# Attention logits of a graph network: four groups' head sums in four quarters of the partitions, and the edges' product filled up with zero rows

## What is computed

```python
x_l = (x @ W_l).reshape(n, H, C)          # H = 8 heads, C = 16
x_r = (x @ W_r).reshape(n, H, C)
e = (ea @ W_e).reshape(-1, H, C)          # ea: 32 features of each edge
m = leaky_relu(x_l[src] + x_r[dst] + e, 0.2)
alpha = einsum('ehc,hc->eh', m, att)      # 8 logits of each edge
amax = segment_max(alpha, dst)
expa = exp(alpha - amax[dst])
out = segment_sum(x_l[src] * a[:, :, None], dst)   # a = expa / sum of expa
```

## Time and profile before

| | |
|---|---|
| time, median of 3 runs | 2102.23 us (2099.22 to 2106.14) |
| the profiled execution: time | 2107.33 us |
| its span, first to last instruction | 2105.5 us |
| mean granted TensorE clock | 0.884 |
| PE busy | 1848.9 us (88%) |
| VectorE busy | 1373.9 us (65%) |
| ScalarE busy | 1035.5 us (49%) |
| GpSimd busy | 844.7 us (40%) |

### The profile page before, as it was taken

How to read it: one execution, slowest core, us unless ns; L and a number is a source line. 1 busy time by engine, 2 the same in 40 slices (tenths; PEclk the granted TensorE clock), 3 DMA queues, 4 the chain that set the end, 5 groups by cost and what they waited for, 6 DMA issues and landing times. The chain is left out here.

```text
span 2105.5 us, 35427 instructions
## 1 busy us (share of the span) xinstructions
PE 1848.9 (88%) x10749; PEld 1210.7 (58%) x10749; DVE 1373.9 (65%) x3215; ACT 1035.5 (49%) x2285; POOL 844.7 (40%) x884
## 2 busy tenths in 40 slices
PE   5677789997999997789999999999999999998856
PEld 2567765556888775335555555555555555555545
DVE  6999967775533335686666666666666666567775
ACT  0588877754642344124545454444545454543325
POOL 2000000001000000577777777777777777775200
PEclk9655569998999999779999999999999999998877
DMA  3100000001520001333333333333333333333111
GB/s 97 43 2 2 2 9 0 1 20 38 148 85 1 6 1 35 92 89 88 97 96 95 94 95 94 94 93 95 94 92 91 93 92 92 96 87 81 34 36 31
DMA packets 132536, 133.24 MB, mean 63 GB/s; under 512 B 29098, under 2 KB 102403, under 8 KB 132355
## 3 DMA queue, kind: packets, MB, share of 16 engines
q1 hardware_dynamic: 104578, 73.76, 12.1%
q0 software_dynamic: 27776, 57.20, 11.1%
HBM read 126.05 MB, written 4.82 MB: 62 GB/s over the span
## 5 line engine op out<-in xcount | busy, mean ns | idle before, releaser
L2203 POOL DMA_INDIRECT rows<-x_l,src x856 | 821.4, 960 | 309.5 <-issue 250.9
L2330 ACT ACTIVATE bent<-psum 128x512 f32<-128x512 f32 x214 | 126.8, 593 | 379.9 <-PE psum L2230 372.8
L2291 PEld LDWEIGHTS psum<-both,node_hot 128*128 128x128 f32 x1712 | 247.0, 209 | 83.2 <-issue 72.6
L2291 PE MATMUL psum<-both,node_hot 128*128 128x144 f32 x1712 | 293.1, 321 | 0.0
L2388 DVE TENSOR_TENSOR bent<-psum,bent 128x512 f32<-128x512 f32 x214 | 147.6, 690 | 195.0 <-ACT bent L2330 194.5
L2345 ACT ACTIVATE apart<-iota,rel 128x128 bf16<-128x128 f32 x796 | 252.9, 388 | 9.2 <-PE psum L2291 7.6
L2221 PEld LDWEIGHTS psum<-hot,x_r_parts 128*128 x1284 | 115.2, 100 | 235.5 <-issue 219.7
L2224 PE MATMUL psum<-edges,w_e 32*128 32x512 f32 x428 | 247.2, 658 | 0.1
L2241 PE MATMUL psum<-bent,att_heads 128*64 128x512 f32 (+2 forms) x428 | 243.8, 665 | 0.0
L2221 PE MATMUL psum<-hot,x_r_parts 128*128 128x256 bf16 x1284 | 187.4, 282 | 50.0 <-DVE hot L2384 49.1
L2481 DVE TENSOR_TENSOR acc<-acc,psum 128x144 f32 x428 | 128.8, 301 | 134.1 <-PE psum L2291 95.9
(11 more groups left out here) (343 smaller groups left out, 2396.7 us busy)
## 6 DMA issues: line engine op xcount, KB each, us to landing
rel_row<-e_rel_rows SPq DMA_DIRECT2D x107, 256.0 KB
edges<-edge_t SPq DMA_DIRECT2D x428, 32.0 KB
rows<-x_l,src POOLq DMA_INDIRECT x856
edge_part<-edge_t SPq DMA_DIRECT2D x40, 320.0 KB, 3.1
ht<-x SPq DMA_DIRECT2D x6, 256.0 KB, 2.8
new<-e_new_before SPq DMA_DIRECT2D x24, 64.0 KB
new<-e_new_behind SPq DMA_DIRECT2D x24, 64.0 KB
x_l<-rows SPq DMA_DIRECT2D x4, 320.0 KB
```

The source lines that it names most:

```text
L2203: e.indirect_dma_start(rows[:, g % ring, j * ROW:(j + 1) * ROW], None, k.xl, bass.IndirectOffsetOnAxis(ap=src[:, at:at + 1], axis=0)).then ...
L2291: final = e.matmul(to, near_hot[:, at, j, :], both[:, at, j, :], start=j % 2 == 0, stop=j % 2 == 1)
```

## The change

1. The head sums of four groups are made together, in one slot: group c of the four goes to its own quarter of the partitions (32 c to 32 c + 31) with a 128 x 32 slice of `att_heads`. A batch of 8 is two such fours; they share a quarter's rows by the shifted slice. So the lines now spread over 128 partitions, of which 64 are in use, and all that works on them takes 128 partitions: scans, maximum, exponential.
2. `bent` has six buffers in place of three.
3. `edges` and `w_e` have 128 rows; rows 32 to 127 are filled with zeros once (two memsets on POOL in the function before, project). The DMAs still bring 32 rows.
4. turn_weights: the transposes become float32 products with `used`, the 64 used columns of the identity; turn_ends and turn_carries write into the bank of the turned weights, not into the lines' bank.
5. `new` is loaded by eight DMAs of 16 lines, not two of 64; DVE clears it once at the start.

```diff
@@ project: POOL @@
                 e.memset(k.att_heads[:, :], 0.0).then_inc(*blank.up())
+                e.memset(w_e[:, :], 0.0).then_inc(*blank.up())
+                e.memset(tables.edges[:, :, :], 0.0)
                 e.wait_ge(kept_r.sem, kept_r.at(5))
@@ project: DVE @@
-                e.wait_ge(blank.sem, blank.at(1))
+                e.wait_ge(blank.sem, blank.at(2))
...
-                        e.tensor_copy(w_e[:, :], raw[0:DE, 2, :]).then_inc(*v.up())
+                        e.tensor_copy(w_e[0:DE, :], raw[0:DE, 2, :]).then_inc(*v.up())
@@ EdgeTables @@
+        self.edges = sb("edges", [P, EDGE_SLOTS, 4 * P])
@@ Batch @@
+        self.quads = [(lo, min(lo + 4, n)) for lo in range(0, n, 4)]
+        self.runs = [(0, n)] if n % 4 == 0 else self.quads
@@ attention @@
-        by_pair, firsts, rows2, loaded = tables.by_pair, tables.firsts, tables.rows2, tables.loaded
-        edges = sb("edges", [DE, edge_slots, 4 * P])
+        by_pair, firsts, rows2, loaded, edges = tables.by_pair, tables.firsts, tables.rows2, tables.loaded, tables.edges
...
-        bent = sb("bent", [P, 3, 4 * P])
+        bent = sb("bent", [P, BENT, 4 * P])
...
         def summed_in(t):
-            ends = [b.over - 1 for b in plan]
-            return [g for g in (t - 2, t - 1) if 0 <= g < groups and (g == t - 1) == (g in ends)]
+            return [(b, lo, hi) for b, lo, hi in quads if t == b.first + hi + (hi < b.n)]
...
+        used = k.ident[:, :].rearrange("p (j q h) -> p j q h", j=4, h=HEADS)[:, :, 0:2, :]
...
         def ends_of(b, j):
-            return bank_of(b)[LINES:LINES + 1, j * P:j * P + b.lines]
+            return weight_bank(b)[0:1, j * P:(j + 1) * P]
@@ SP @@
                         if b.i >= 2:
                             e.wait_ge(less.sem, less.at(3 * (b.i - 1)))
+                        else:
+                            e.wait_ge(blank.sem, blank.at(1))
                         for j in range(2):
-                            e.dma_start(new[0:b.lines, b.two, j, :], by_head(j, b)).then_inc(*new_here[b.two].up(16))
+                            for column in range(4):
+                                of = by_head(j, b, column)
+                                e.dma_start(new[32 * column:32 * column + HEADS * of.shape[0], b.two, j, :],
+                                            of).then_inc(*new_here[b.two].up(16))
@@ PE @@
-                def head_sums(g):
...
-                    e.wait_ge(leaky.sem, leaky.at(g + 1))
...
-                    e.matmul(alphas_of(b), k.att_heads[:, low:low + b.lines], bent[:, g % 3, :],
-                             start=c == 0, stop=c == b.n - 1).then_inc(*alphas.up())
+                def head_sums(b, lo, hi):
+                    low = LINES - HEADS - 2 * lo
+                    e.wait_ge(leaky.sem, leaky.at(b.first + hi))
...
+                    for c in range(lo, hi):
+                        column = 32 * (c - lo)
+                        final = e.matmul(alphas_of(b)[column:column + 32, :], k.att_heads[:, low:low + 32],
+                                         bent[:, (b.first + c) % BENT, :], start=lo == 0, stop=c + 4 >= b.n)
+                    final.then_inc(*alphas.up())
...
-                    for j in range(4):
-                        e.transpose(bank[:, j * LINES:j * LINES + b.lines], trial[0:b.lines, b.two, 1, j * P:(j + 1) * P],
-                                    k.ident[0:b.lines, 0:b.lines]).then_inc(*back.up())
...
+                    for j in range(8):
+                        of = trial[:, b.two, 1, j * P:(j + 1) * P] if j < 4 else last[:, b.two, (j - 4) * P:(j - 3) * P]
+                        e.matmul(bank[:, j * LINES:(j + 1) * LINES], of, used, start=True, stop=True).then_inc(*back.up())
@@ DVE @@
+                e.memset(new[:, :, :, :], 0.0).then_inc(*blank.up())
+                e.memset(taken[:, :, :], 0.0).then_inc(*v.up())
                 e.memset(acc[:, :, :], 0.0).then_inc(*v.up())
```

More of the change, by code:

```diff
@@ L2001, in __init__ @@
         self.i, self.first, self.n = i, first, n
-        self.over, self.two, self.lines = first + n, i % 2, n * HEADS
+        self.over, self.two = first + n, i % 2
+        self.quads = [(lo, min(lo + 4, n)) for lo in range(0, n, 4)]
+        self.runs = [(0, n)] if n % 4 == 0 else self.quads
 def batches(groups):
@@ L2040, in attention @@
     steps = 2 * s.padded
-    ring, slots, edge_slots, deep, lag = RING, 6, 3, 4, TOGETHER_ROWS + 6
+    ring, slots, edge_slots, deep, lag = RING, 6, EDGE_SLOTS, 4, TOGETHER_ROWS + 6
     wide = D + 2 * HEADS
@@ L2072, in new_rows, with quads_by, moves_by @@
     def new_rows(b):
-        return 16 * 2 * sum(a.two == b.two and a.i <= b.i for a in plan)
+        return 16 * 2 * 4 * sum(a.two == b.two and a.i <= b.i for a in plan)
+    quads = [(b, lo, hi) for b in plan for lo, hi in b.quads]
+    def quads_by(g):
+        return sum(b.first + lo <= g for b, lo, _ in quads)
+    def moves_by(i):
+        return sum(2 + 2 * len(b.runs) for b in plan[:i])
     with ExitStack() as scope:
@@ L2125, in alphas_of, with by_head, by_group, in_quads @@
         def alphas_of(b):
-            return bank_of(b)[0:b.lines, :]
-        def by_head(j, b):
-            return k.e_new[j][b.first:b.over, :].rearrange("c (o e) -> c o e", o=1).to_broadcast([b.n, HEADS, 4 * P])
+            return bank_of(b)
+        def by_head(j, b, column):
+            of = k.e_new[j][b.first + column:b.over:4, :]
+            return of.rearrange("c (o e) -> c o e", o=1).to_broadcast([of.shape[0], HEADS, 4 * P])
+        def by_group(row, lo, hi):
+            return row.rearrange("p (j q h) -> p h q j", j=4, h=HEADS)[:, :, lo // 4:-(-hi // 4), 0:min(4, hi - lo)]
+        def in_quads(x):
+            return x.rearrange("p h (q j) -> p h q j", j=min(4, x.shape[2]))
+        used = k.ident[:, :].rearrange("p (j q h) -> p j q h", j=4, h=HEADS)[:, :, 0:2, :]
         def rows_at(g):
@@ L2263, in turn_weights, with turn_carries @@
                         e.wait_ge(filled.sem, filled.at(plan[b.i - 2].over))
+                    for j, at in enumerate((4 * P - 1, 0)):
+                        e.wait_ge(trials.sem, trials.at(2 * b.i + j + 1))
+                        e.matmul(ends_of(b, j), trial[:, b.two, j, at:at + 1], k.ident[:, :],
+                                 start=True, stop=True).then_inc(*lines_here.up())
+                def turn_carries(b):
+                    e.wait_ge(chained.sem, chained.at(moves_by(b.i + 1) - 1))
+                    for j in range(2):
+                        e.matmul(carries_of(b)[:, j:j + 1], taken[:, j, :], k.ident[0:1, 0:1],
+                                 start=True, stop=True).then_inc(*carries_here.up())
+                def turn_weights(b):
                     e.wait_ge(exps.sem, exps.at(2 * b.i + 1))
@@ L2299, in _ @@
                         join(t)
-                    for g in summed_in(t):
-                        head_sums(g)
+                    for b, lo, hi in summed_in(t):
+                        head_sums(b, lo, hi)
                     if t + 1 < groups:
@@ L2387, in bend @@
                     e.wait_ge(sloped.sem, sloped.at(g + 1))
-                    e.tensor_tensor(bent[:, g % 3, :], z_banks[g % 2], bent[:, g % 3, :], ALU.max).then_inc(*leaky.up())
+                    at = bent[:, g % BENT, :]
+                    e.tensor_tensor(at, z_banks[g % 2], at, ALU.max).then_inc(*leaky.up())
                 def scan(b, j, initial):
-                    to, at, what = trial[0:b.lines, b.two, j, :], new[0:b.lines, b.two, j, :], alphas_of(b)
+                    to, at, what = trial[:, b.two, j, :], new[:, b.two, j, :], alphas_of(b)
                     if j:
@@ L2416, in scan_ends @@
                             what = what[:, :, ::-1]
-                        e.tensor_copy(taken[:, j, 0:b.lines].rearrange("p (c h) -> p h c", h=HEADS), what).then_inc(*chained.up())
+                        for lo, hi in b.runs:
+                            e.tensor_copy(by_group(taken[:, j, :], lo, hi), in_quads(what[:, :, lo:hi])).then_inc(*chained.up())
                     e.tensor_copy(line[:, 0, :, 0], chain[:, 0, :, b.n]).then_inc(*chained.up())
```

69 lines of the change are left out of this document (27 added, 42 removed).

## The result

| | before | after |
|---|---|---|
| time, median (range), 5 runs each | 2104.73 us (2099.22 to 2106.38) | 2088.67 us (2087.26 to 2091.26) |
| the profiled execution: time, span | 2107.33, 2105.5 | 2087.26, 2085.4 |
| mean granted clock | 0.884 | 0.888 |
| first gather | 855.6 | 852.7 |
| first gather to join 198 | 1043.7 | 1015.4 |

The ratio is 0.993 [0.9913, 0.9946]: 16 us faster, where 44 were forecast. The last four rows add up to the spans, and their differences are -2.9, -28.3, +7.0 and +4.1, together -20.1. The first is spread of the layers before (the first gather came between 851.0 and 855.2 in other executions). So the long stretch brought 28 us, and the end lost 11 of them again. The profiled execution before was the slowest of its five, so the spans differ by 20 us and the medians by 16.

What follows compares the result with a forecast made beforehand. PE was taken as the bound at 41.25 us a batch, with POOL's floor of 40.1 close below. The long stretch's -42 and the end's -2 made -44 from 2102.2: 2058 us, range 2040 to 2090.

Steps and rivals of the forecast that it cites:

- POOL's floor: Gathers in the long stretch: POOL needs 1071.3 us whatever PE does, 5.01 us a group, 40.1 us a batch of eight.
- -42 at the join of group 198: End of the long stretch: with POOL as the bound, PE's join of group 198 comes 42 us earlier, at 1857.
- The end, forecast at -2: Short batches from group 198 on: PE savings against SP's added loads change the end by 0 (-10 to +8), taken as -2.
- +3 for SP: SP's queue at the end: six more loads of new delay edges by 0 to 2 us in three batches, 1 taken each.
- After it nothing changes: Piece behind the short batches' stretch (groups 198 to 213): no change in time.
- rival 1: PE's clock: waits in every slot bring half clock, PE's batch 40 or 41 us; total 2067 to 2087; chance 0.2.
- PE's batch, 37.8: PE's time per batch of eight in the long stretch falls from 41.25 to 37.8 us (34.3 to 42.0).
- q: PE time of one four of head sums on the quarters: taken as 2.3 us, between 1.0 and 3.6.
- No overlap (2): Head sums' four products do not run at once: q 3.6, PE's batch 40.4 us, total 2082 to 2102; chance 0.12.
- bare weight loads (3): Quarters' weight loads do not run beside products: q over 4.3, slower, total 2130 to 2180; chance 0.07.
- A better end (4): Without group 198's lag and with q 1.0, the end shortens by 10 to 15 us: 2040 to 2048; chance 0.1.
- The slack granted to DVE, ACT, `bent` and the memsets: Scans and copies over 128 partitions cost the same, six buffers never stall, memsets (up to 1.7 us, 1.3 us) are covered.

Runs made afterwards that it cites:

- With POOL out of the way: Changed kernel with the fourth of each group's gathers not issued from group 24 on (output differs): 1968.51 us, ratio 0.9351 to the kernel before.
- zero rows alone: Kernel before with only edges and w_e at 128 rows, 96 of them zeros: 2070.87 us, ratio 0.9847 without pauses; 0.9925 with pauses.
- late `new`: Changed kernel with edges and rel_row fetched ahead of SP's eight loads of new: 2081.56 us, ratio 0.9903 to the kernel before without pauses; 1.0016 with.
- the quarters alone: Changed kernel with the edges' product again on 32 rows: 2088.98 us, ratio 0.9926 to the kernel before without pauses; 1.0109 with pauses.

## Why the prediction was right or wrong

**What bounds the kernel: right.** "PE sets the pace, but only 40 us lie between it and a floor that the change does not touch." PE was the bound, by about 1 us a batch, and POOL is now.

**POOL's floor: the first step that failed.** "Only 38.2 + 2.3 = 40.5 us is waiting for PE or DVE. So POOL needs 1111.8 - 40.5 = 1071.3 us." The 0.3 us between two gathers is there also when POOL waits, but then it is counted under what it waited for. With it in every one of the 855 gaps (250.9 / 823 = 0.3049 each), 260.7 us can't go; the idle time before was 250.9 + 40.5 = 291.4, so only 30.7 could. After, it is 256.1 + 4.6 = 260.7, just this. Besides, the gathers took 827.5 us in place of 821.4. So the floor is 1087 us and not 1071, 5.08 us a group and not 5.01: 10 us of that is the gap, 6 the longer gathers. turn_ends recur every 40.4 us and not 40.1 (20 batches, 1035.05 to 1843.24). The term of the sum that this sets, -42 at the join of group 198, measured -31. That join came 1015.4 us after the first gather where 1001.4 were forecast: 14 of the 24 us by which the profiled execution missed the forecast (the end is 13, and the earlier start gave 3 back).

**The end, forecast at -2: the second step that failed.** It was +11. "+3 for SP" had the right mechanism, and was named as the likeliest failure; it measured 6 to 7. The price of a load was about right (0.69 taken, 0.65 measured), but the step allowed 0 to 2 us in each of three batches, and PE's three waits for `edges` were 9.6 us in total, up to 3.9 each, with 6.1 us more of VectorE's for `rel_row`. "After it nothing changes" was wrong: the last two turn_weights stand behind the last join on the path that sets the end, and the term was charged only in the four short batches before. It measured 4.0 to 4.6. The end's range went up to +8, and +11 lies outside it. That the total lies within 2040 to 2090, by 1 us, is luck: the upper bound had been set for rival 1, which did not happen.

**PE's batch, 37.8: too long by 3.3, without effect.** With POOL out of the way it was 34.5. q was taken as 2.3 and measured 1.00, the lower bound: all four products run at once, and the trace's two records of each run one behind the other. The edges' product gave 0.29 a slot, over the 0.2 taken and near the bound of 0.3. turn_weights was +1.1, not +1.4. The prediction said that nearly the same time follows for any q below 3.4, and that held: with zero rows alone, one head sum at a time, the long stretch was no longer than with the quarters.

**The pages cited.** The Trainium skill ("TensorE: Matmul & The Clock Gate", Part 3) gives 2.38 times the speed for three products on column quarters; here four ran in 1.00 us, the time of one. It also says there that weight loads overlap with products in flight only where the row groups differ; here four loads of 109 ns each ran beside the products on the same row group. In both the measurement decides. The drain at a change of tiling mode that the Trainium skill states ("TensorEngine Tiling (Array Packing)", Key Properties) fits what was seen: leaving the 32-row form saved 0.19 and 0.10 us a slot. No run separates the drain from other costs of that form. By itself this part was worth 33 us, and the quarters 15.

**The rivals.** The clock (1): no, the clock was 0.95 in the window at 1500 and POOL no longer waited for PE. Its time of 2067 to 2087 came near for another reason. Without the zero rows the clock did fall, to 0.81 to 0.89. No overlap (2) and bare weight loads (3): both fell with q = 1.00; nothing came out slower. A better end (4): no, the end is where it was lost. The slack granted to DVE, ACT, `bent` and the memsets held: in the long stretch PE's waits for DVE are no longer than before (20.0 us for `hot` after 29.9, and 18.5 for the chained scan after 21.2).

## What to carry to other kernels

Where one engine has a fixed gap between its instructions, count that gap in every interval, those with waits too, before its floor is worked out: here it was 10 of 40 us. When a change makes the bound engine faster than the next one, its cheapest part can be enough, and every cost that the rest puts elsewhere (queue issues, work after the last step) is then paid from nothing; try the parts alone. A tail after the main loop needs its own sum for each added instruction, since nothing there hides it.

## What was not expected of the hardware

- Four float32 products on four column quarters, with the same 128 rows, ran in 1.00 us, the time of one.
- Filling the contraction side from 32 to 128 rows with zeros made a product of 512 columns 0.19 us shorter and the products ahead of it 0.10, from start to start.
- A load over 16 lines held the SP queue about as long (0.65 us) as one over 32 (0.69).
- Eight products with 64 rows of weights in place of eight transposes were followed by half clock in each batch looked at, 1.6 us more in the next three pieces of work; with 128 rows of weights they were not.
- On some chips POOL's gathers stopped for some 2 us, 68 to 104 times in an execution, most often 11.8 us apart, and VectorE and ScalarE had waits of a kind that the traces of the other chips don't show. With zero rows alone, VectorE, then POOL, at one such moment (PE stood idle for 1.85 us there, too):

```profile
1309.94 0.69 DVE L2464 TENSOR_TENSOR both<-rows,psum 128x512 f32<-128x512 f32 x1 [4.15 <-remote]
```

```profile
1310.26 0.95 POOL L2206 DMA_INDIRECT rows<-x_l,src  x1 [2.32 <-DMA w<-L_gnn_W_self_t]
```

From 900 on such waits took 189.0 us of POOL's time there, in 99 times. The releaser named is a load of a layer long past, so it doesn't tell what ended the pause.

**What stays open:** the cause of the pauses, and why versions with the quarters gained nothing on such chips (1.00 to 1.01) while those with zero rows did (0.98 to 0.99). The traces show this much: on such a chip POOL waited for PE again, 70 us with zero rows alone, 110 with the changed kernel's late `new` and 174 with the quarters alone, at a granted clock of 0.91, 0.84 and 0.79 from 1200 to 2000, so PE held POOL up again, and its clock was lower with the quarters; why, they don't show. Open are also some 3 us before join 198 and 3 behind it that neither SP's loads nor the bare turn_weights explain; the 6 us more of the gathers; and what sets the half clock behind certain products.
